# A two-layer decoder with routed experts on one core: the first nine expert blocks issued behind the first stream's last attention, six of them in one PSUM bank, with new issue orders

## The chip, the cores and the metric

The kernel runs on one core of one Trainium2 chip. The metric is the device time of one execution in microseconds (us), lower is better. The core has five engines that run side by side: PE (TensorE, matmuls), DVE (VectorE), ACT (ScalarE), POOL (GpSimd) and SP (SyncE, which issues DMAs). Each has a queue of its own and works through it strictly in order; they wait for each other on semaphores.

## The reference, cut to what matters

Tokens: 32 sequences of 64 with 128 features. Six sublayers run one after the other, each ending in a residual sum and a layer norm. The last one is a mixture of experts:

```python
x = _layernorm(x + _L0_attn_ref(...))      # causal attention, 16 heads of 8
x = _layernorm(x + _L0_xattn_ref(...))     # attention over ctx, normed heads
x = _layernorm(x + _L0_ffn_ref(...))       # fp4-quantized gated FFN
x = _layernorm(x + _L1_attn_ref(...))      # convolutions, linear attention, MLP
x = _layernorm(x + _L1_xattn_ref(...))     # causal attention over ctx
x = _layernorm(x + _L1_ffn_ref(...))       # experts

# _L1_ffn_ref
router_probs = softmax(residual @ W_router)                    # 8 experts
top_k_probs, top_k_idx = top_k(router_probs, 2)
top_k_probs = top_k_probs / (sum(top_k_probs) + 1e-08)
gate = silu(residual @ W_gate[e] + b_gate[e]); up = residual @ W_up[e] + b_up[e]
expert_out = (gate * up) @ W_out[e] + b_out[e]                 # 256 hidden
output = sum over e of expert_weights[e] * expert_out[e]
```

All is fp32.

## The kernel before, in words

The 2,048 tokens are four chunks of 512. Two streams, `first` and `second`, each take two of them in two turns, so that two chunks are in work at the same time. Each stream owns four of the eight PSUM banks (`h.ps`, banks 0 to 3 of its half) and its own SBUF tiles. On each engine three generators exist: the network of the first stream, the network of the second, and the expert blocks. A list of counts per engine, `ORDER`, says how many steps of each are issued in turn (`weave`, the third count is the blocks'); since the queues are in order, this list is the schedule. A step is what lies between two `yield`s.

A stream's turn ends with `causal_cross_attention` (four tiles: scores, row maxima, exponentials, transposes of the probabilities, mix with the values, projection, norm) and `routing`. Routing takes the logits (PE L941), the softmax and the two best experts (DVE L1709 to L1729), ranks the tokens of each expert with matmuls (L950, L953), writes each token's row with shares (L1736, L1739), then the token's place in its expert's list (L1751 to L1760); the counts so far are in `next_row` (L1755, semaphore step "taken"). The shares are transposed (PE L962), copied (ACT L1260) and mixed with the output bias (PE L967), and DVE adds this to the token's row (`h.acc`, L1763). POOL sends the rows to a table in HBM by indirect DMAs, eight for a stream's turn (L1998). `plan_blocks` (DVE L1800 to L1824) works out from the counts which expert and which 128 rows each block has.

There are 39 expert blocks of 128 rows. Their plan is made in three phases: blocks 0 to 8 are known once the first turn of both streams is counted, 9 to 16 after the first stream's second turn, 17 to 38 after the second's. For a block `b`: SP loads 128 rows (L536, six slots `xb`), PE transposes them (`turn`, L976), ACT copies (`take`, L1267), DVE copies the expert's weights (`weigh`, L1871; it loads the expert's number into a register first, L1867), PE projects (`gate_up`, L984, eight matmul passes into bank 1 or 2 in alternation), ACT applies Silu (`gate`, L1274), DVE multiplies with the up half (`hide`, L1879), PE makes the output (`out_part`, L998, bank 3), ACT scales it (`take_out`, L1284) and POOL sends it to HBM by an indirect DMA (L2007). DVE also works out the places for three blocks at a time (`pick`, L1839 to L1861). Between blocks 16 and 17 PE loads the sums so far into the second stream's banks (`add_base`, L1017). At the end the shares are read back, added (L1043) and normed.

The blocks use the first stream's tiles: `xb` lies in `first.probs`, the transposed rows, gates and hidden values in `first.pT`, the outputs in `first.qT`, the weights in `first.k4`, and PSUM banks 0 to 3 are the first stream's. In the kernel before, no block touches them before the first stream's last routing is over: SP and DVE wait for all of its `route_dve` steps, DVE also for its `route_pe` and `route_act`, and on PE block 0's projection stands behind the routing of both streams.

Of the kernel before, what the change touches and what calls it, by code (L numbers as in the profile page):

```python
# [26 lines left out]
ACT = mybir.ActivationFunctionType  # L27
# [4 lines left out]
P = 128  # L32
# [20 lines left out]
DEPTH, YDEPTH, WDEPTH, BATCH = 6, 4, 3, 3  # L53

# [38 lines left out]
def steps(*names):  # L93
# [49 lines left out]
    "act": (  # L143
# [11 lines left out]
    "dve": (  # L155
# [1994 lines left out]
```

## Time and profile before

| | us |
|---|---|
| median of 3 runs | 739.48 |
| lowest, highest | 736.78, 741.73 |
| span of the profiled execution | 763.12 |
| PE busy in it | 568.6 (75%) |
| DVE busy | 531.9 (70%) |
| ACT busy | 327.7 (43%) |
| POOL busy | 200.5 (26%) |

The profile is of one execution, and its times are positions on that execution's clock from the start of its span. PEld is the weight load of PE. "Granted clock" is the share of full speed that TensorE was allowed: 0.50 is 1.2 GHz and 1.00 is 2.4 GHz. "Issue" as the reason of a wait means that the profile shows nothing that the engine waited for, "remote" or "an unknown queue" that a semaphore came without a known sender close by.

### The profile page before, as it was taken

What the parts mean: (1) busy time and instruction counts of PE and PEld (TensorE: products, weight loads), DVE (VectorE), ACT (ScalarE), POOL (GpSimd) and SP (SyncE); (2) the same over time, 40 slices, a digit from 0 to 9 for tenths busy, and PEclk for the clock granted to TensorE, in tenths of its full rate; (3) what the DMA queues carried; (4) which work ended last, traced back from release to release, by engine and by line L of the source; (5) the groups of instructions that cost most, each with busy time, mean ns of one, the idle gap of its engine ahead of it and who ended that gap; (6) DMA issues with size and microseconds to landing.
All of it is one profiled execution on the core that took longest, in us unless ns stands there. A gap on an engine that the chain in (4) does not pass through costs nothing.

```text
span 763.1 us, 13948 instructions
## 1 busy us (share of the span) xinstructions
PE 568.6 (75%) x4890; PEld 393.2 (52%) x4890; DVE 531.9 (70%) x1520; ACT 327.7 (43%) x642; POOL 200.5 (26%) x312
## 2 busy tenths in 40 slices
PE   5787668756788688775975784667886987679984
PEld 2466546534455347442764463444542675567861
DVE  9667677888667667673686778996855767455633
ACT  2653445312474465142634451126744632344632
POOL 2204201201203502046043011121024034454543
PEclk9897669667699989687888797777997885599998
DMA  9993000000000000011000000000000001132215
GB/s 276 326 298 98 28 1 2 1 0 0 2 1 0 1 1 3 1 33 54 2 6 0 1 2 1 0 2 0 2 0 1 2 1 40 58 96 68 78 54 155
DMA packets 45556, 32.34 MB, mean 42 GB/s; under 512 B 4281, under 2 KB 43457, under 8 KB 45361
## 3 DMA queue, kind: packets, MB, share of 16 engines
q1 hardware_dynamic: 41104, 25.49, 12.1%
q0 software_dynamic: 2272, 4.92, 1.9%
q10 hardware_dynamic: 2112, 1.05, 0.5%
q8 instruction: 40, 0.66, 0.4%
q14 instruction: 28, 0.22, 0.1%
HBM read 13.83 MB, written 17.62 MB: 41 GB/s over the span
## 4 chain that ended last, share of the span: by engine, by line
PE 43%; DVE 32%; ACT 11%; issue 7%; POOL 4%; another core or an unknown queue 2%; DMA 1%; DVEq 0%; ACTq 0%; POOLq 0%
PE ps L643 5%; PE ps L984 5%; PE ps L624 5%; PE ps L687 5%; DVE s_row_max L1408 2%; PE ps L998 2%; ACT s_probs L1135 2%; DVE s_probs L1413 2%; DVE s_r L1377 2%; PE ps L655 2%; PE ps L906 1%; PE ps L911 1%; DVE s_st L1380 1%; DVE s_work L1367 1%
## 5 line engine op out<-in xcount | busy, mean ns | idle before, releaser
L1954 POOL TENSOR_TENSOR s_rs<-s_mv,eps 128x1 f32<-128x1 f32 x80 | 17.1, 215 | 349.3 <-DVE s_mv L1383 349.2
L1408 DVE TENSOR_REDUCE s_row_max<-ps 128x16 f32<-128x1024 f32 x48 | 58.7, 1222 | 62.3 <-PE ps L643 47.2
L1115 ACT ACTIVATE s_pT<-ps 128x512 f32<-128x512 f32 x96 | 55.5, 594 | 56.6 <-PE ps L624 44.2
L624 PE MATMUL ps<-tabs,s_probs 128*128 128x128 f32 x384 | 64.2, 302 | 19.8 <-ACT s_probs L1135 12.2
L643 PE MATMUL ps<-s_k,s_q 64*64 64x256 f32 x768 | 64.8, 451 | 13.5 <-ACT s_q L1085 9.9
L624 PEld LDWEIGHTS ps<-tabs,s_probs 128*128 128x128 f32 x384 | 45.8, 152 | 40.7 <-issue 19.9
L1135 ACT ACTIVATE s_probs<-s_probs 128x1024 f32<-128x1024 f32 x48 | 50.6, 1055 | 24.0 <-DVE s_probs L1413 23.7
L1413 DVE TENSOR_TENSOR s_probs<-ps,s_row_max 128x1024 f32<-128x1024 f32 x48 | 58.7, 1222 | 1.3
L687 PE MATMUL ps<-s_v,s_pT 128*64 128x18 f32 x1536 | 54.9, 216 | 3.5 <-issue 1.4
L687 PEld LDWEIGHTS ps<-s_v,s_pT 128*64 128x64 f32 x1536 | 51.0, 143 | 12.0 <-issue 11.0
L984 PE MATMUL ps<-s_pT,s_k 128*128 128x128 f32 x312 | 48.4, 304 | 3.8 <-issue 1.6
L1985 POOL TENSOR_SCALAR s_k<-s_kT,tabs 128x512 f32<-128x512 f32 x24 | 38.1, 1596 | 45.9 <-DVE s_kT L1442 28.8
L2007 POOL DMA_INDIRECT shares_io<-s_qT,y_row x39 | 38.0, 975 | 42.5 <-ACT s_qT L1284 38.1
L643 PEld LDWEIGHTS ps<-s_k,s_q 64*64 64x64 f32 x768 | 32.2, 156 | 31.1 <-issue 13.5
L984 PEld LDWEIGHTS ps<-s_pT,s_k 128*128 128x128 f32 x312 | 42.9, 213 | 8.4 <-issue 6.5
L1957 POOL TENSOR_TENSOR s_rs<-s_rs,minus_half 128x1 f32<-128x1 f32 x80 | 44.9, 565 | 5.2
L1879 DVE SCALAR_TENSOR_TENSOR s_pT<-ps,s_k,s_pT 128x128 f32<-128x128 f32 x78 | 23.7, 345 | 28.2 <-ACT s_pT L1274 19.8
L1274 ACT ACTIVATE s_pT<-ps,s_k 128x128 f32<-128x128 f32 x78 | 24.5, 367 | 37.7 <-PE ps L984 22.8
L1998 POOL DMA_INDIRECT rows_io<-s_work,s_slot x32 | 31.3, 977 | 16.7 <-issue 9.2
L1065 ACT ACTIVATE s_xT<-ps 128x512 f32<-128x512 f32 x20 | 11.9, 594 | 49.3 <-PE ps L603 24.4
L809 PE MATMUL ps<-gu_w,s_xT 128*128 128x352 f32 x64 | 30.8, 625 | 1.1 <-ACT s_xT L1065 1.1
L998 PE MATMUL ps<-wo,s_pT 128*128 x156 | 27.1, 298 | 5.6 <-ACT s_qT L1284 5.6
(288 smaller groups left out, 1247.8 us busy)
## 6 DMA issues: line engine op xcount, KB each, us to landing
rows_io<-zero_rows SPq DMA_DIRECT2D x9, 1152.0 KB, 11.9
s_probs<-rows_io SPq DMA_DIRECT2D x39, 72.0 KB
s_xin<-in_x SPq DMA_DIRECT2D x4, 256.0 KB, 4.1
s_cin<-in_ctx SPq DMA_DIRECT2D x4, 256.0 KB, 4.1
wgu<-in_wg SPq DMA_DIRECT2D x1, 1024.0 KB
wgu<-in_wu SPq DMA_DIRECT2D x1, 1024.0 KB
wo<-in_wo SPq DMA_DIRECT2D x1, 1024.0 KB
out_x<-s_work SPq DMA_DIRECT2D x4, 256.0 KB, 2.3
```

The lines of the kernel that those rows point to most:

```text
L624: ins = pe.transpose(h.ps[:, 2, tile(j)], h.probs[:, t % 2, 8 * part + 2 * j:8 * part + 2 * j + 2, :] .rearrange("p h k -> p (h k)"), ident)
L643: ins = pe.matmul(h.ps[S * b:S * b + S, half, 256 * side:256 * side + 256], h.q4[rows, side, S * sq:S * sq + S], h.k4[rows, sq, :, :].rear ...
L687: ins = pe.matmul(h.ps[S * b:S * b + S, 3, 18 * j:18 * j + 18], h.pT[:, t % 2, j, S * b:S * b + S], h.v2[:, 2 * t + b, 2 * j:2 * j + 2, :] ...
L984: ins = pe.matmul(ps[:, 1 + b % 2, tile(m)], wb[:, b % WDEPTH, tile(m)], xbT[:, b % 2, :], start=True, stop=True)
L998: ins = pe.matmul(ps[:, 3, 0:P], bhid[:, b % 2, tile(m)], wo[:, bass.ds(e, 1), m, :].rearrange("p e d -> p (e d)"), start=m == 0, stop=m == 1)
L1115: act.activation(h.pT[:, t % 2, 4 * part:4 * part + 4, :].rearrange("p j q -> p (j q)"), h.ps[:, 2, :], ACT.Copy).then_inc(h.pT_here.sem, 1)
L1135: act.activation(h.probs[:, u % 2, :, :], h.probs[:, u % 2, :, :], ACT.Exp).then_inc(h.exped.sem, 1)
L1408: dve.tensor_reduce(h.row_max[:, t % 2, :], s3, AX, ALU.max).then_inc(h.max_here.sem, 1)
L1413: dve.tensor_tensor(h.probs[:, t % 2, :, :], s3, h.row_max[:, t % 2, :].rearrange("p (h o) -> p h o", o=1).to_broadcast([P, H, S]), ALU.su ...
L1957: pool.tensor_tensor(h.rs[:, t % 2:t % 2 + 1], h.rs[:, t % 2:t % 2 + 1], minus_half[:, 0:1], ALU.pow).then_inc(h.rstd_here.sem, 1)
L1985: ins = pool.tensor_scalar(h.k4[:, :, m, :], seqs(h.kT[:, :]), tab("member")[:, m:m + 1], None, ALU.mult)
L2007: pool.indirect_dma_start(shares_io, bass.IndirectOffsetOnAxis(ap=y_row[:, g % 3, k:k + 1], axis=0), yb[:, b % YDEPTH, :], None).then_inc( ...
```

## The change

It does six things.

- SP's first load of a block waits for `first.p_turned` of the last turn (all probabilities of the first stream transposed) instead of `first.route_dve`.
- PE's first projection waits for `first.shifted` (banks 0 and 1 read), the first output for `first.summed` (bank 3 read), and projection 6 for all of the first stream's `route_dve`. ACT's first copy and DVE's first weighing wait for `first.mixed`.
- Blocks 0 to 5 all project into bank 1 (`NARROW = 6`), blocks from 6 on alternate as before. A projection therefore waits for the hide of the block before it up to block 6, and of the one two before from block 7 on.
- In its last turn, the first stream's shares are transposed and mixed in its bank 2 instead of 3, and the transposes wait for the step "taken" instead of "rows".
- `ewT` (the transposed shares) moves from `k4` to `work`, since `wb` needs its place.
- The four lists in `ORDER` are new throughout. On PE, `turn` of blocks 0 and 1 stands between the last tiles of both attentions, projection 0 directly behind the first stream's bias mix, and then, in turns with the second stream's ranks, shares and bias mix, projections 1 and 2. On DVE the weighings of blocks 0 and 1 stand inside the routings; the hide of block 0 stands in front of the larger part of the plan of blocks 9 to 16 and of the second stream's counts and slots, whose steps follow between the hides of blocks 0 to 5; the plan of the last phase ends behind the weighing of block 14 instead of 16. On POOL six of the first stream's sends come first, then the second stream's first, and then those left alternate with the blocks' own sends up to block 9; before, the sends of both streams came first but for three.

```diff
+NARROW = 6
@@ ORDER: all four lists are new @@
-            h.ewT = placed(h.k4, 3 * TOK, TOK)[0:EXPERTS, :]
+            h.ewT = placed(work, 3 * TOK, TOK)[0:EXPERTS, :]
+        def proj_bank(b):
+            return 1 if b < NARROW else 1 + b % 2
+        def bank_free(b):
+            return b if b <= NARROW else b - 1
+        def share_bank(h):
+            return 2 if h is first and h.turn == PASSES - 1 else 3
@@ sync, blocks_of_experts @@
-                        sp.wait_ge(*first.route_dve.at(0, PASSES))
+                        sp.wait_ge(*first.p_turned.at(0, PASSES))
@@ tensor, routing @@
-                pe.wait_ge(*h.route_dve.at(ROUTE_DVE["rows"]))
+                pe.wait_ge(*h.route_dve.at(ROUTE_DVE["taken" if share_bank(h) == 2 else "rows"]))
-                    ins = pe.transpose(h.ps[0:EXPERTS, 3, tile(t)], h.pay[:, t, P:P + EXPERTS], ident)
+                    ins = pe.transpose(h.ps[0:EXPERTS, share_bank(h), tile(t)], h.pay[:, t, P:P + EXPERTS], ident)
-                    ins = pe.matmul(h.ps[:, 3, tile(t)], h.ewT[:, tile(t)], bout[:, :], start=True, stop=True)
+                    ins = pe.matmul(h.ps[:, share_bank(h), tile(t)], h.ewT[:, tile(t)], bout[:, :], start=True, stop=True)
@@ tensor, gate_up and out_part @@
-                    if b >= 2:
-                        pe.wait_ge(b_hid, b - 1)
+                    if b == 0:
+                        pe.wait_ge(*first.shifted.at(0, PASSES))
+                    if b == NARROW:
+                        pe.wait_ge(*first.route_dve.at(0, PASSES))
+                    if bank_free(b):
+                        pe.wait_ge(b_hid, bank_free(b))
-                        ins = pe.matmul(ps[:, 1 + b % 2, tile(m)], ...)
+                        ins = pe.matmul(ps[:, proj_bank(b), tile(m)], ...)
-                    if b >= 1:
+                    if b == 0:
+                        pe.wait_ge(*first.summed.at(0, PASSES))
+                    else:
                         pe.wait_ge(yb_here, b)
@@ scalar, blocks_of_experts; ps[:, proj_bank(b)] in gate as well @@
                 yield
+                act.wait_ge(*first.mixed.at(0, PASSES))
                 take(0)
@@ vector, blocks_of_experts; ps[:, proj_bank(b)] in hide as well @@
-                dve.wait_ge(*first.route_dve.at(0, PASSES))
-                dve.wait_ge(*first.route_pe.at(0, PASSES))
-                dve.wait_ge(*first.route_act.at(0, PASSES))
+                dve.wait_ge(*first.mixed.at(0, PASSES))
                 weigh(0)
```

## Rows read from the trace of the kernel before

**Rows 1.** Busy time by stretch: stretch, length, busy us (instructions) by engine, clock, DMA.

```profile
625.00:640.00 15.00, 11.31 (x60) 8.86 (x58) 10.08 (x71) 2.61 (x6) 2.17 (x6) 0.50 0.01 2
...
650.00:660.00 10.00, 3.49 (x14) 2.96 (x14) 2.65 (x12) 2.70 (x10) 4.76 (x5) 0.50 0.17 54
...
690.00:745.00 55.00, 49.32 (x339) 39.31 (x338) 28.80 (x105) 25.99 (x94) 25.36 (x26) 1.00 0.25 72
```

**Rows 2.** The chain that ended last, 600 to 763 us: start, us, what.

```profile
647.86 1.71 PE ps L984 x8
649.56 5.34 issue
...
675.16 2.23 another core or an unknown queue
...
678.04 1.53 another core or an unknown queue
...
691.23 3.44 PE ps L1017 x8
```

**Rows 3.** Timeline, the handover: start, us, engine, line, operation, [idle before <-releaser].

```profile
613.13 0.63 PE L624 MATMUL ps<-tabs,s_probs 128*128 128x128 f32 x4 [0.23 <-ACT s_pT L1115]
...
634.41 0.19 DVE L1739 TENSOR_TENSOR s_work<-s_spread 128x32 f32<-128x32 f32 x1
...
635.43 1.01 PE L962 MATMUL ps<-tabs,s_work 128*8 128x128 f32 x4
...
636.69 0.16 DVE L1755 TENSOR_TENSOR next_row<-next_row,ps 128x8 f32<-128x8 f32 x1
...
637.12 2.07 PE L967 MATMUL ps<-bout,s_k 8*128 8x128 f32 x8 [0.68 <-ACT s_k L1260]
...
639.62 1.06 POOL L1998 DMA_INDIRECT rows_io<-s_work,s_slot  x1 [7.53 <-DVE s_slot L1760]
...
641.48 0.17 DVE L1805 TENSOR_TENSOR fp_gu<-fp_gu,taken 128x8 f32<-128x8 f32 x1
...
642.44 0.21 DVE L1811 TENSOR_REDUCE fp_gu<-fp_gu 128x8 f32<-128x56 f32 x1
...
645.66 1.98 PE L984 MATMUL ps<-s_pT,s_k 128*128 128x128 f32 x8
...
646.20 1.28 ACT L1274 ACT_TABLE_LOAD   x1
...
652.37 0.63 ACT L1274 ACTIVATE s_pT<-ps,s_k 128x128 f32<-128x128 f32 x2 [4.88 <-remote]
...
655.01 0.96 POOL L1998 DMA_INDIRECT rows_io<-s_work,s_slot  x1 [0.30 <-issue]
```

**Rows 4.** The weighing's lines: line, engine, operation, count, ns min/median/max, first and last start.

```profile
L1867 DVEq TENSOR_LOAD <-plan_expert x21: 298/304/547, 644.0 to 698.8; - x21
L1867 DVEq FUSED_REGOPS x21: 190/190/216, 644.6 to 699.2; - x21
...
L1871 DVE TENSOR_SCALAR s_k<-wgu x39: 428/431/679, 645.0 to 733.5; 128x516 f32 x39
```

**Rows 5.** Timeline of single blocks: block 3, then projections 6 and 38.

```profile
660.10 2.05 PE L984 MATMUL ps<-s_pT,s_k 128*128 128x128 f32 x8 [0.63 <-ACT s_pT L1267]
...
662.19 0.63 ACT L1274 ACTIVATE s_pT<-ps,s_k 128x128 f32<-128x128 f32 x2 [2.13 <-PE ps L984]
...
663.11 0.61 DVE L1879 SCALAR_TENSOR_TENSOR s_pT<-ps,s_k,s_pT 128x128 f32<-128x128 f32 x2 [1.22 <-PE ps L998]
...
666.73 1.13 PE L984 MATMUL ps<-s_pT,s_k 128*128 128x128 f32 x8
...
734.24 1.13 PE L984 MATMUL ps<-s_pT,s_k 128*128 128x128 f32 x8 [0.21 <-issue]
```

**Rows 6.** Busy time by stretch in the first turn's routing (columns as in rows 1).

```profile
341.00:347.00 6.00, 6.00 (x48) 3.14 (x41) 3.00 (x3) 1.74 (x3) 4.69 (x5) 0.51 0.17 52
347.00:363.00 16.00, 6.90 (x55) 3.54 (x54) 4.31 (x5) 3.09 (x5) 9.61 (x10) 0.82 0.15 51
```

More of the change, by code:

```diff
@@ L980, in gate_up @@
                     pe.wait_ge(b_weights, b + 1)
-                    if b >= 2:
-                        pe.wait_ge(b_hid, b - 1)
+                    if b == 0:
[4 more added lines that the diff above has]
+                        pe.wait_ge(b_hid, bank_free(b))
                     for m in range(2 * EM // P):
-                        ins = pe.matmul(ps[:, 1 + b % 2, tile(m)], wb[:, b % WDEPTH, tile(m)], xbT[:, b % 2, :], start=True, stop=True)
+                        ins = pe.matmul(ps[:, proj_bank(b), tile(m)], wb[:, b % WDEPTH, tile(m)], xbT[:, b % 2, :], start=True, stop=True)
                     ins.then_inc(b_proj, 1)
@@ L1259, in routing @@
                 act.wait_ge(*h.route_pe.at(ROUTE_PE["shares_turned"]))
-                act.activation(h.ewT[:, :], h.ps[0:EXPERTS, 3, 0:TOK], ACT.Copy).then_inc(h.route_act.sem, 1)
+                act.activation(h.ewT[:, :], h.ps[0:EXPERTS, share_bank(h), 0:TOK], ACT.Copy).then_inc(h.route_act.sem, 1)
             def blocks_of_experts():
@@ L1273, in gate @@
                     for m in range(EM // P):
-                        ins = act.activation(bsg[:, b % 2, tile(m)], ps[:, 1 + b % 2, tile(m)], ACT.Silu,
+                        ins = act.activation(bsg[:, b % 2, tile(m)], ps[:, proj_bank(b), tile(m)], ACT.Silu,
                                              bias=wb[:, b % WDEPTH, 2 * EM + m:2 * EM + m + 1])
@@ L1762, in routing @@
                 dve.wait_ge(*h.route_pe.at(ROUTE_PE["bias_mix"]))
-                dve.tensor_tensor(h.acc[:, :, :], h.ps[:, 3, :].rearrange("p (t d) -> p t d", d=P), h.pay[:, :, 0:P],
+                dve.tensor_tensor(h.acc[:, :, :], h.ps[:, share_bank(h), :].rearrange("p (t d) -> p t d", d=P), h.pay[:, :, 0:P],
                                   ALU.add).then_inc(h.route_dve.sem, 1)
@@ L1878, in hide @@
                     for m in range(EM // P):
-                        ins = dve.scalar_tensor_tensor(bhid[:, b % 2, tile(m)], ps[:, 1 + b % 2, EM + P * m:EM + P * m + P],
+                        ins = dve.scalar_tensor_tensor(bhid[:, b % 2, tile(m)], ps[:, proj_bank(b), EM + P * m:EM + P * m + P],
                                                        wb[:, b % WDEPTH, 2 * EM + 2 + m:2 * EM + 3 + m], bsg[:, b % 2, tile(m)], ALU.add, ALU.mult)
```

110 rows, old and new, of the table ORDER are left out of this document.

## The prediction

> **What bounds the kernel now.** I read the busy times by stretch first, then the chain of waits, then the timeline around the place where the network hands over to the expert blocks. The stretches [rows 1] show three regimes. From 625 to 640 us both streams route: PE runs at a granted clock of 0.50 (1.2 GHz) and DVE is busy 10.1 of 15 us with tiny steps. From 650 to 660 us nothing is full: PE 3.5 of 10 us, DVE 2.7, ACT 2.7. From 690 to 745 us the clock is 1.00 (2.4 GHz) and PE is busy 49.3 of 55 us, so there PE is the bound. The first projection starts at 645.66 and the last (block 38) at 734.24; block 3 starts at 660.10 [rows 3, 5], so 35 blocks take 74.1 us, 2.1 us each, but the first three take 14.4 us. The chain of waits names the hole: 5.34 us of idle after block 1's projection, 2.23 and 1.53 us near 676 us that end with no known releaser, and 3.44 us of the eight matmuls that bring the base into PSUM between blocks 16 and 17 [rows 2]. So the change can win only between about 635 and 665 us; what it wins there is kept, since PE works back to back behind it.
>
> The hole is odd: block 0's projection ends at 647.64, the table load for Silu at 647.48, yet ACT begins the gate at 652.37 [rows 3]. The wait between them is on PE's own semaphore, which arrived 4.7 us late. At that time POOL issues 13 row sends back to back, 639.62 to 655.97. In the first turn it is alike: while 15 sends run from 340.6 us on, PE keeps 6.0 of 6 us busy at first, then 6.9 of 16 [rows 6]. I call this late release; it goes with a long run of sends, and begins some 7 us into one.
>
> **The change part by part.**
> 1. *Loads and turns.* SP loads blocks behind the last transpose of the first stream's probabilities instead of behind its last routing step, so the first six 72 KB loads move from 641 us to about 615 us, just behind those transposes (613.13 to 613.76 [rows 3]), where POOL sends nothing. The transposes of blocks 0 and 1 and their copies (PE 0.47 and ACT 0.28 us each, cold) now stand inside the tail of both attentions, in front of work that is on the path. Cost +0.5 us, between 0 (they fit in gaps) and 1.5.
> 2. *The first stream's routing.* Its last shares go through bank 2, which is free only when the row counts were taken (L1755, ends 636.85) instead of when the rows are there (L1739, ends 634.60) [rows 3]. With the weighing of block 0 put into DVE before it, I put that at 637.1. From the shares' transposes (L962) to the bias mix (L967) it is 1.69 us and the mix lasts 2.07 [rows 3]: it ends at 640.9, and block 0's projection, now next on PE and no longer behind the second stream's mix, starts there: 4.8 us earlier than 645.66. The Silu table load is hidden, since ACT is free from about 639 us.
> 3. *One bank for six blocks.* Each of projections 1 to 6 must wait until the block before has been hidden. Block 3 shows such a round, cold: projection from 660.10, gate from 662.19, hide from 663.11 to 663.72 [rows 5]: 3.62 us. Warm it is 1.13 + 0.63 + 0.61 us and small gaps, 2.5 us.
> 4. *DVE.* The new order puts 24 steps of routing and planning, 7 of picking, 5 weighings and 5 hides between the hides of blocks 0 and 5. A step costs 0.24 us (from 641.48 to 642.44, four of them [rows 3]); a weighing 1.1 us with its register load (0.30 + 0.19 + 0.43 us and gaps [rows 4]); a hide 0.61 [rows 5]; the accumulate with the mix adds 0.4. Sum 31 x 0.24 + 5 x 1.1 + 5 x 0.61 + 0.4 = 16.4 us. These steps are not new work: before, they ran ahead of the first hide or in the hole, and cost nothing there. Now they are beside the blocks.
>    Block 0 is hidden at 640.9 + 3.6 = 644.6 (DVE's own queue gives the same). Projection 6 then starts between 644.6 + 16.4 = 661.0 (DVE decides) and 644.6 + 5 x 3.62 = 662.7 (the one bank decides, cold), and was at 666.73 [rows 5]: 4.0 to 5.7 us earlier. The second stream's mix (2.07 us) now stands between projections 1 and 2 and speaks for the late end. I take 4.3 us.
> 5. *Late releases.* Those gains are against a trace with 5.34 us of hole in it, while my rounds have none. The 16 sends are still issued, and blocks now run beside all of them. In the new POOL order the second stream's first send waits for slots that DVE writes only behind the hide of block 2, so the run is six sends long, then pauses, then mixes with the blocks' own sends. Bounds: nothing returns (0) or all of it (+5.3). Since the 7 us of grace cover the first run and not what follows, I take half, +2.7.
> 6. *Plan of the last phase.* It ends two blocks earlier in DVE's order. Hidden anyway: PE loads the base for 3.44 us between blocks 16 and 17 [rows 2] and block 17's transpose follows directly. I take 0; if that cover were gone it would be worth about 2 us, a block's pace.
> 7. *Orders elsewhere.* Nearly every line of the four orders is rewritten, but step by step they are close: no step of PE changes its place by more than five among 631, ACT's by four; DVE's by up to 20 among 1,326 and POOL's by up to 12. Sum 0, with +-4 us for what a reordered DVE does to two streams over 625 us.
>
> Sum: +0.5 - 4.3 + 2.7 = -1.1 us against the profiled 763.1, so 762.0. That execution is 23.6 us above the median of the runs. I can't say where those lie; if the late releases are partly of the profiled execution alone, the old hole is smaller in the runs. The difference is carried over as it stands: 739.48 - 1.1 = 738.4, and I say **738 us**.
>
> The Trainium skill ("SBUF — State Buffer", SBUF: two separate sides) says that GpSimd and VectorE share a port pair under an exclusive lock, so that a DVE fp32 copy in a fast mode keeps POOL from writing descriptors, and puts a POOL DMA overlapped by one at about 3.1 us instead of 0.62. By its figures the nine weighings beside sends would cost some 2.5 us each on POOL. The traced sends beside the weighings at 645.02 and 646.57 kept their 1.27 us rhythm, so the trace does not show this size.
>
> **Rivals.**
> A. *The hole is closed (chance 0.20).* The long run of 13 sends is what makes the semaphores late, and the new order breaks it at six. Then term 5 is 0 and the two later stalls (2.23 and 1.53 us) go too, as B's last sends are spread: 738.4 - 2.7 - 3.8 = 732; if the denser PE also brings the clock to 1.00 sooner than at 664 us, rounds of 2.5 us and DVE's 16.4 decide, 1.5 more: 730. For it: early loads don't collide. Against: the stall at 677 us comes after only four indirect DMAs in a row.
> B. *Blocks in the way (0.20): slower.* The second stream's routing now queues behind projections 0 and 1, gates 0 and 1 and three hides, each of which can be released late. Two or three late releases of 4.7 us, each in a loop where one bank lets nothing overlap, are 9.4 to 14 us, less the 4.3 won: 743 to 749, say 745. It decides from the point where more than one such release falls in the six one-bank rounds.
> C. *It does nothing (part of the forecast's neighbourhood, 0.15).* In a run with no late releases before, block 0 would have been gated at 647.7 and hidden by 649.0, projection 2 would have followed at once and projection 3 one cold round later, near 652.7; one more cold round and two of the steady pace of 2.1 put projection 6 near 660.5 on the trace's clock, as early as the new order brings it. Only term 1 and a little of the denser DVE queue are left: 740.
> D. *The rewritten orders decide (0.10),* 4 us or more to either side, 733 or 744.
> The forecast itself, 735 to 741, has 0.35.
>
> **How the numbers follow.** The range takes A's 730 and B up to 747: 729 to 747, leaving out 0.1 on each side. About 1%, 7.4 us, is what a measurement of this kernel tells from no change: under 732.1 is faster, over 746.9 slower. Faster: A, most of its reach, and a part of D and of the forecast's tail, 0.23. Slower: the upper half of B and of D with a little for what I don't see, 0.17. Within 1%: 0.60.
>
> **What would show it.** Right: the first L984-type projection near 641 with the first stream's mix directly before it; the distance from projection to projection 3.0 to 3.6 us for blocks 0 to 6 and 2.1 behind; projection 6 near 662 on the old clock. Term 3 is wrong if DVE is idle before those hides, term 4 if it is not and the rounds are shorter than 3 us. Term 5 shows as ACT waits of over 1 us that begin after a projection has ended, while POOL sends. The prediction is wrong if the network's end has moved by more than 4 us before the blocks, or if the second stream's sends land so late that block 17 waits for its load.

## The result, and the profile after

| | us |
|---|---|
| kernel before, median | 738.32 |
| changed kernel, median of 4 runs | 758.04 |
| lowest, highest of them | 754.86, 760.19 |
| ratio, 95% interval | 1.027, 1.022 to 1.032 |
| span of its profiled execution | 756.5 |

The change costs 19.7 us. The prediction, 738 us with a range of 729 to 747, was wrong in its sign and outside its range.

One thing has to be settled before the traces are compared. The profiled execution of the changed kernel (756.5) agrees with its runs. That of the kernel before (763.12) stood 23.6 us above its own median, and some 2 us more as a run, since a run's time is 2.0 us above its span (758.46 and 756.5 for the changed kernel's profiled run). So the changed kernel's trace is 6.6 us shorter than the trace of before, although the kernel is 19.7 us slower. Busy time by stretch of the changed kernel, at the places that answer to [rows 6] and [rows 1] (columns as there):

```profile
356.00:372.00 16.00, 14.24 (x233) 9.96 (x233) 11.87 (x14) 10.47 (x16) 6.79 (x8) 1.00 0.11 38
635.70:650.70 15.00, 9.86 (x52) 7.66 (x51) 11.47 (x78) 4.06 (x8) 4.45 (x8) 0.62 0.02 7
660.70:670.70 10.00, 6.45 (x51) 5.88 (x51) 7.58 (x35) 4.15 (x16) 7.67 (x8) 1.00 0.21 65
683.40:738.40 55.00, 49.58 (x351) 40.51 (x349) 29.74 (x108) 26.80 (x98) 29.36 (x31) 1.00 0.26 78
```

Both holes of the trace of before are gone. Beside the sends of the first turn PE is busy 14.2 of 16 us (6.90 in [rows 6]), and among the first blocks 6.5 of 10 us (3.49 in [rows 1]). The steady part is as it was, 49.6 of 55 us at a clock of 1.00.

The timeline of the handover in the changed kernel (start, us, engine, line, operation, [idle before <-releaser]). L1773 is L1751 of before, where the first stream's rows are known; L1003 is L984; L1295 is L1274; L1901 is L1879:

```profile
645.20 0.18 DVE L1773 TENSOR_TENSOR s_row_of<-ps,next_row 128x32 f32<-128x32 f32 x1
...
649.40 2.08 PE L1003 MATMUL ps<-s_pT,s_k 128*128 128x128 f32 x8
...
651.51 0.62 ACT L1295 ACTIVATE s_pT<-ps,s_k 128x128 f32<-128x128 f32 x2 [2.87 <-PE ps L1003]
652.17 0.61 DVE L1901 SCALAR_TENSOR_TENSOR s_pT<-ps,s_k,s_pT 128x128 f32<-128x128 f32 x2
...
652.93 1.20 PE L1003 MATMUL ps<-s_pT,s_k 128*128 128x128 f32 x8 [0.16 <-DVE s_pT L1901]
...
655.57 1.13 PE L1003 MATMUL ps<-s_pT,s_k 128*128 128x128 f32 x8 [0.26 <-DVE s_pT L1901]
...
666.35 1.13 PE L1003 MATMUL ps<-s_pT,s_k 128*128 128x128 f32 x8 [0.90 <-DVE s_pT L1901]
```

The handover does what the diff says. Block 0 is projected 4.2 us behind L1773, behind 11.1 us in the trace of before, and the six blocks follow in one-bank rounds, each projection released by the hide ahead of it. But L1773 stands at 645.20, where L1751 stood at 634.5: the network arrives 10.7 us late, although the trace of before has 12.8 us of late semaphores ahead of that place (e1 below). Against ordinary executions of the old order it is twice as much: the profiled executions of e10 and e14 below, with spans of 735.1 and 735.9 us, have that operation at 623.41 and 623.82, so 21.8 and 21.4 us earlier. The loss lies ahead of everything that the prediction worked out.

To compare handovers, take that operation, the first stream's row places, as the mark. "Cold" stands for a granted clock of 0.50 (1.2 GHz), "warm" for 1.00. Per profiled execution, in us (first column: where it starts on the clock; the others: from there to the projections of four blocks and to the end of the span):

| kernel | mark | block 0 | block 6 | block 9 | block 17 | end |
|---|---|---|---|---|---|---|
| before, first profile | 634.5 | 11.1 | 32.2 | 37.8 | 60.9 | 128.6 |
| before, profiled again (e1) | 632.7 | 11.2 | 22.5 | 28.1 | 45.8 | 111.9 |
| changed | 645.2 | 4.2 | 21.2 | 27.4 | 46.2 | 111.3 |

### The profile page after: what moved, and what is told of

Read it like the earlier page. It is cut to its first block, busy times and chain, and to the rows that moved or that the text cites. A ratio compares the mean times of both kernels' runs of the same rounds, so it can differ in the third digit from the quotient of the medians.

```text
span 756.5 us, 13948 instructions
## 1 busy us (share of the span) xinstructions
PE 568.0 (75%) x4890; PEld 391.5 (52%) x4890; DVE 526.6 (70%) x1520; ACT 326.8 (43%) x642; POOL 199.9 (26%) x312
## 4 chain that ended last, share of the span: by engine, by line
PE 49%; DVE 27%; ACT 11%; issue 6%; POOL 3%; DMA 2%; SPq 0%; DVEq 0%; POOLq 0%; ACTq 0%
PE ps L702 6%; PE ps L658 5%; PE ps L639 5%; PE ps L1003 3%; DVE s_row_max L1430 2%; PE ps L625 2%; PE ps L921 2%; PE ps L1019 2%; PE ps L926 2%; DVE s_probs L1435 2%; PE ps L670 2%; ACT s_probs L1156 2%; PE ps L824 1%; DVE s_r L1399 1%; ACT s_q L1106 1%
## 5 line engine op out<-in xcount | busy, mean ns | idle before, releaser
L1974 POOL TENSOR_TENSOR s_rs<-s_mv,eps 128x1 f32<-128x1 f32 x80 | 16.4, 208 | 338.1 <-DVE s_mv L1405 337.9
L639 PE MATMUL ps<-tabs,s_probs 128*128 128x128 f32 x384 | 62.3, 293 | 23.0 <-ACT s_probs L1156 20.0
L658 PE MATMUL ps<-s_k,s_q 64*64 64x256 f32 x768 | 61.1, 442 | 10.1 <-ACT s_q L1106 10.1
L639 PEld LDWEIGHTS ps<-tabs,s_probs 128*128 128x128 f32 x384 | 44.0, 147 | 41.8 <-ACT s_probs L1156 29.1
L2005 POOL TENSOR_SCALAR s_k<-s_kT,tabs 128x512 f32<-128x512 f32 x24 | 37.8, 1587 | 48.7 <-DVE s_kT L1464 29.5
L1003 PE MATMUL ps<-s_pT,s_k 128*128 128x128 f32 x312 | 44.2, 286 | 6.3 <-DVE s_pT L1901 4.2
L1003 PEld LDWEIGHTS ps<-s_pT,s_k 128*128 128x128 f32 x312 | 38.7, 195 | 11.4 <-issue 5.9
L2027 POOL DMA_INDIRECT shares_io<-s_qT,y_row x39 | 38.0, 974 | 23.6 <-ACT s_qT L1305 20.0
L658 PEld LDWEIGHTS ps<-s_k,s_q 64*64 64x64 f32 x768 | 30.6, 154 | 25.6 <-ACT s_q L1106 11.2
L1295 ACT ACTIVATE s_pT<-ps,s_k 128x128 f32<-128x128 f32 x78 | 24.4, 364 | 31.6 <-PE ps L1003 31.6
L670 PE MATMUL ps<-mats,s_headsT 128*128 128x128 f32 x96 | 24.7, 353 | 12.2 <-DVE s_heads L1448 9.4
L1901 DVE SCALAR_TENSOR_TENSOR s_pT<-ps,s_k,s_pT 128x128 f32<-128x128 f32 x78 | 23.7, 346 | 11.8 <-ACT s_pT L1295 8.1
```

Of the source, the lines that this page charges most:

```text
L639: ins = pe.transpose(h.ps[:, 2, tile(j)], h.probs[:, t % 2, 8 * part + 2 * j:8 * part + 2 * j + 2, :] .rearrange("p h k -> p (h k)"), ident)
L658: ins = pe.matmul(h.ps[S * b:S * b + S, half, 256 * side:256 * side + 256], h.q4[rows, side, S * sq:S * sq + S], h.k4[rows, sq, :, :].rear ...
L670: pe.matmul(h.ps[:, 3, P:2 * P], h.headsT[:, u % 2, :], mat(w_out), start=True, stop=True).then_inc(h.projected.sem, 1)
L1003: ins = pe.matmul(ps[:, proj_bank(b), tile(m)], wb[:, b % WDEPTH, tile(m)], xbT[:, b % 2, :], start=True, stop=True)
L2027: pool.indirect_dma_start(shares_io, bass.IndirectOffsetOnAxis(ap=y_row[:, g % 3, k:k + 1], axis=0), yb[:, b % YDEPTH, :], None).then_inc( ...
```

## The experiments

Two questions are told apart: where the network loses its time (e1, e3, e5 to e7, e9 to e11), and where the gain of the handover goes (e1, e2, e4, e8, e12 to e14). The theories before the first runs: **U**, the new orders of the network ahead of the last attentions cost it; **B**, the blocks stand in the way of the second stream's routing (rival B of the prediction); **E**, the edits cost it, whatever the order.

### e1: the kernel before, profiled again

No edit.

> The kernel before, unchanged, profiled once more. Theory U (the new orders of the first 590 us cost about 20 us, and the execution that the prediction read was an untypical one, with some 12 us of late semaphores at 342 to 362 us and some 12 more at 647 to 665 us): time 739, and if this profile agrees with its runs its span is about 737, the step that stood at 362 us in the first profile stands near 350, and projection 38 near 710. Theory B (the blocks stand in the way of the second stream's routing, so the loss lies behind 620 us): the time is 739 too, and against this profile the changed kernel loses nothing before 620 us and some 20 us behind it.

Measured: median 738.11 us over 10 runs, against 737.90 of before. The profiled execution has a span of 744.5; its run, 746.54, is the longest of the ten (the shortest is 733.90) and has the lowest mean clock of them, 0.828. Its busy times by stretch, at the places of the two holes, then its timeline:

```profile
355.00:371.00 16.00, 14.76 (x226) 10.35 (x223) 13.27 (x16) 10.82 (x16) 10.45 (x11) 0.99 0.17 56
...
648.00:658.00 10.00, 9.48 (x76) 8.99 (x77) 8.20 (x35) 5.99 (x24) 7.78 (x8) 0.96 0.29 89
```

```profile
643.82 1.97 PE L984 MATMUL ps<-s_pT,s_k 128*128 128x128 f32 x8
...
645.82 0.62 ACT L1274 ACTIVATE s_pT<-ps,s_k 128x128 f32<-128x128 f32 x2 [0.18 <-PE ps L984]
```

The same kernel, the same 16 sends, and no hole: block 0 is gated 0.03 us after its projection ended, not 4.73 us as in [rows 3]. The late semaphores belong to the one execution that was profiled first. The longest of them stands in the first turn: an 11.3 us wait of ACT from 350.75 on, without a known sender. Operation by operation, the first profile loses 12.8 us against this one between 340 and 362 us and 16.7 us behind the mark; this one in turn is 9.0 us slower ahead of 340 us, where its granted clock is lower. The expected place of projection 38, 710, was 715.2, by that lower clock. That e1 is a long run does not touch the comparison behind the mark: e10 and e14 have the old order there too, and put block 0 at 11.1, block 6 at 22.5, block 9 at 28.0 and the end at 111.7 and 112.1.

### e2 to e4: orders and edits apart

```diff
# e2 (base: changed kernel)
-ORDER = the new lists
+ORDER = the lists of before
# e3 (base: before)
-ORDER = the lists of before
+ORDER = steps of each stream's network ahead of its last attention as in the new lists, the rest as before
# e4 (base: changed kernel)
-ORDER = the new lists
+ORDER = steps of each stream's network ahead of its last attention as before, the rest as in the new lists
```

> The changed kernel with all its new waits, the one bank and the new place of the shares, but with the four issue orders of the kernel before. Theory U: 739 to 742, since the network is issued as before; the first block is projected behind both routings and only the six blocks in one bank can cost 1 to 3 us. Theory E (the edits themselves cost it: one bank for six blocks, the shares' wait for the row counts): 750 to 758. Theory B: like U here, since no block stands ahead of the second stream's routing.

> The kernel before (old waits, two banks) with the new issue order for every step of the network that stands ahead of the last attention of each stream, and the old order from there on. Theory U: 756 to 762, all of the loss and nothing of the gain. Theory B and theory E: 737 to 742, as the kernel before.

> The changed kernel with the old issue order for every step of the network that stands ahead of the last attention of each stream, and the new order from there on (both last attentions, both routings, the blocks). Theory U: 733 to 738, the gain of the handover without the loss upstream, and so a version better than both. Theory B and theory E: 755 to 760, as the changed kernel.

| | median us | ratio to before | mark | end behind the mark |
|---|---|---|---|---|
| e2, edits, old orders | 744.08 | 1.012 (1.002 to 1.022) | 621.7 | 119.0 |
| e3, new orders upstream alone | 759.66 | 1.029 (1.021 to 1.037) | 644.0 | 112.6 |
| e4, edits and new orders behind | 739.64 | 1.000 (0.995 to 1.006) | 621.2 | 113.5 |

Theory U holds. The kernel before with nothing but new orders upstream has all of the loss (+21.8 us), and the changed kernel without them can't be told from before. B falls twice: e4 has the blocks in front of the second stream's routing and loses nothing, and in the changed kernel the second stream's rows (second L1773, 652.82) follow the first's after 7.6 us, as they do in e1 (7.8). E is right for a smaller sum: with the old orders the edits cost 6.2 us (interval 0.2% to 2.2%), most of it in the one bank. There block 0 starts 1.2 us later behind the mark than in e1, and block 6 8.8 us later: the rounds of the first blocks are 4.0, 3.5 and 3.8 us (projections at 634.01, 637.97, 641.47, 645.23), almost wholly cold (mean clock 0.55). e4 did not gain the 4 us that theory U as written promised.

### Where the network loses it: e6, e7, e9

Comparing e3 with e4, operation by operation, the delay of e3 grows at many places, roughly from 2 us at 160 to 5 at 240, 9 at 320, 15 at 380, 19 at 460 and 25 at 540; at the mark it is 22.8. The execution of e4 has a high mean clock (0.872), and 2.3 us of this are its lead over e10. Theory **M**: many local changes of order, each paid where it stands. Theory **S**: one place, or a state carried along.

```diff
 ORDER (base: before; all four engines)
# e6
+steps of the first turn of both streams as in the new lists
# e9
+steps of the second turn ahead of its last attention as in the new lists
# e7
+steps of the linear block, in both turns, as in the new lists
```

> The kernel before with the new order for all steps of the first turn (both streams, its routing included) and the old order for everything else. Theory M (the loss is made of many local changes of order, each paid where it stands): 746 to 750, the 9 to 10 us that the changed kernel is late at 340 us. Theory S (one place, or the state the second turn is entered in, carries the loss): either 738 or 758.

> The kernel before with the new order for the steps of the second turn ahead of its last attention, and the old order for the first turn and for the rest. Theory M (many local places, each paid where it stands): what is left of the 21.5 us of the whole upstream order when the first turn's 5.9 us are taken off, 15 to 16 us, so 751 to 755. If the two halves do not add up (under 748 or over 757) the turns act on each other, through the clock or through how far one stream is ahead of the other.

> The kernel before with the new order for the steps of the linear block alone, in both turns. Theory M: between the changed and the former order the stretches that hold these blocks differ by 3.7 us in the first turn and 3 to 4 in the second, so 743 to 747. Theory S: as the kernel before, 738, since the rest of the order is the old one.

| | median us | above before |
|---|---|---|
| e6, first turn | 744.01 (ratio 1.010, 1.004 to 1.016) | 5.9 |
| e9, second turn | 752.84 (1.017, 1.010 to 1.023) | 14.5 |
| e7, linear block, both turns | 742.81 (1.007, 1.004 to 1.010) | 4.7 |

The two halves add up, 5.9 + 14.5 = 20.4 against 21.8 for both, and one sublayer of five holds 4.7. M holds; e6 came out 2 us under its expected range, e7 0.2 us. Each part costs less than 2%, but all three intervals lie above 1.

What a place looks like is seen in the busy times of three pairs of stretches that hold the same work. e4 (old order), then e3 (new order):

```profile
265.00:300.00 35.00, 30.18 (x444) 20.75 (x443) 24.21 (x42) 21.66 (x33) 3.32 (x7) 0.90 0.01 1
300.00:340.00 40.00, 29.01 (x225) 18.30 (x225) 29.66 (x128) 13.98 (x28) 10.56 (x15) 0.81 0.05 14
365.00:400.00 35.00, 24.01 (x280) 20.42 (x280) 29.16 (x92) 13.17 (x28) 15.07 (x21) 0.90 0.01 4
```

```profile
270.10:306.70 36.60, 30.64 (x444) 20.94 (x443) 24.97 (x41) 21.62 (x33) 3.29 (x7) 0.91 0.01 1
306.70:349.80 43.10, 34.52 (x215) 21.86 (x211) 29.89 (x128) 12.24 (x26) 10.47 (x15) 0.68 0.05 13
375.80:415.00 39.20, 28.49 (x275) 24.30 (x275) 27.05 (x92) 12.60 (x26) 16.19 (x23) 0.70 0.03 9
```

In the first pair the clock is alike (0.90, 0.91) and 1.6 us go, 1.1 of them as idle time of PE. In the two others 3.1 and 4.2 us go and the granted clock falls from 0.81 to 0.68 and from 0.90 to 0.70: PE is busy 5.5 and 4.5 us longer with the same work (the counts differ a little, since stretches cut it at different places and some matmul records are missing).

The runs show how much goes with the clock. Over 90 runs of before, all those beside the experiments and e1's, the mean granted clock went from 0.828 to 0.865 and the time followed it by -3.2 us for each 0.01, with 741.5 at 0.84. The changed kernel's four runs (mean clock 0.8375) lie 15.5 us above that line; the other 4 us go with the lower clock (mean of before 0.849). This is a division, not a cause: whether the clock falls first or the waits come first is not shown by it. The same line has something to say on e4. Its ten runs had a higher clock (0.857) and lie 5.0 us above the line, so that its equal time is not an equal handover.

### e5 and e11: one swap of neighbours

```diff
 ORDER["dve"] (base: before), second turn, linear block
-first stream: second tap of the convolution; second stream: norm statistics
+second stream: norm statistics; first stream: second tap of the convolution
```

> The kernel before with two neighbours on DVE exchanged, once: in the second turn's linear block the second stream's norm statistics (four L1596, 0.88 us) are issued ahead of the first stream's second convolution tap (L1589), as the new order has it. In the new order's traces this stands at the head of a place where 3 us go. Theory Q (queue and clock together): ACT's next operation on that tile comes 0.7 us later, PE waits for it over 2 us instead of 1.5, falls to a granted clock of 1.2 GHz, its next two pairs of 128x512 matmuls take 2.07 and 1.91 us instead of 1.13 and 1.02, and DVE's L1620 starts 1.5 to 1.8 us later than before against the tap ahead of the swap (6.1 us behind it before). Theory N (a swap of neighbours costs at most its own length): 0 to 0.7 us later and no slower matmuls. In both the whole kernel stays within its noise, 736 to 742; the trace decides.

The timeline of e4, which has the old order here (L1609 is the tap, L1616 the statistics):

```profile
509.00 0.74 DVE L1605 SCALAR_TENSOR_TENSOR s_work<-s_work,cols 128x504 f32<-128x504 f32 x1 [0.46 <-ACT s_work L1226]
509.78 0.74 DVE L1609 SCALAR_TENSOR_TENSOR s_work<-s_work,cols 128x504 f32<-128x504 f32 x1
510.44 0.88 DVE L1616 BATCH_NORM_STATS2 s_nst<-ps 128x6 f32<-128x128 f32 x4
...
511.24 1.13 PE L864 MATMUL ps<-s_work,mats 128*128 128x512 f32 x2 [1.46 <-ACT s_work L1232]
512.21 1.02 PE L865 MATMUL ps<-s_work,mats 128*128 128x512 f32 x2
...
515.12 0.69 DVE L1640 SCALAR_TENSOR_TENSOR s_kT<-s_k,s_kT 128x512 f32<-128x512 f32 x1 [0.53 <-ACT s_k L1238]
```

The timeline of e5 (the same operations stand at L1584, L1595, L1588, L850, L851 and L1619):

```profile
513.42 0.74 DVE L1584 SCALAR_TENSOR_TENSOR s_work<-s_work,cols 128x504 f32<-128x504 f32 x1 [0.45 <-ACT s_work L1206]
514.08 0.88 DVE L1595 BATCH_NORM_STATS2 s_nst<-ps 128x6 f32<-128x128 f32 x4
514.88 0.72 DVE L1588 SCALAR_TENSOR_TENSOR s_work<-s_work,cols 128x504 f32<-128x504 f32 x1
...
516.32 1.50 PE L850 MATMUL ps<-s_work,mats 128*128 128x512 f32 x2 [2.30 <-ACT s_work L1212]
517.62 1.92 PE L851 MATMUL ps<-s_work,mats 128*128 128x512 f32 x2
...
520.57 0.69 DVE L1619 SCALAR_TENSOR_TENSOR s_kT<-s_k,s_kT 128x512 f32<-128x512 f32 x1 [1.83 <-ACT s_k L1218]
```

Theory Q holds in its mechanism. The tap is 0.7 us later, PE waits 2.30 instead of 1.46 us, and then works at 1.2 GHz: a pair that took 1.02 us takes 1.92. DVE's next dependent operation comes 7.15 us behind the tap ahead of the swap instead of 6.12, a loss of 1.0 us (1.5 to 1.8 was expected). All 16 profiled executions have these two pairs of matmuls. In ten of them PE waited 1.29 to 1.65 us ahead of the first pair, and the pairs took 1.12 or 1.13 and then 1.02 us; in the six others (changed, e3, e5, e7, e9, e11) it waited 1.99 to 2.65 us, and they took 1.44 to 2.08 and then 1.62 to 1.92 us. A little further on two more pairs run slowly, at 531.06 and 532.76 for 1.91 and 1.64 us where e4 has 1.02, and from 528.6 on e4's clock every DVE operation is 2.7 us later than before the swap, to 0.01 us. So one swap of two neighbours, which moves 0.7 us of work, cost 2.7 us at its place. Not all of it stays. Against e10 and e14, which have the old order here and behind it, e5 is 0.7 and 0.3 us late ahead of the swap, 3.4 and 3.0 behind it, but 2.1 and 1.7 at the mark (625.55 against 623.41 and 623.82): 1.2 us came back, between 573 and 614 us on e10's clock. The run itself, 741.26, can't show so little.

e11 takes the swap out of the changed kernel again, and with it POOL's order at the start of the second turn:

```diff
 ORDER (base: changed kernel)
-"dve", that place: statistics, tap
+"dve", that place: tap, statistics
-"pool", first turn's row sends and the next norms: new order
+"pool", first turn's row sends and the next norms: order of before
```

> The changed kernel with two places of its order put back: the DVE swap of e5, and POOL's order of the first turn's row sends and the norms beside them (the place of e10). Theory M: 2.7 us for the first, as e5's trace shows, and 2 to 4 us for the second come back of the 19.7: 751 to 755. Theory S (whatever is put back, the streams fall into the same slower pattern): 757 to 760.

Measured: 754.01 us, 4.0 below the changed kernel, within the expected range; but the four runs of each overlap (750.36 to 758.72, 754.86 to 760.19), so the trace has to carry it. The delay against e4 jumps by 1.5 us at the place of the swap, where e3's jumps by 4.4: 2.9 us came back there. Directly, the changed kernel is 0.5 us ahead of e11 up to the swap and 2.7 behind it from then to the mark (645.20 against 642.48): here nothing of it is made up. At POOL's place, near 370 us, the delay of e11 against e4 jumps by 4.0, as e3's does, and its distance from the changed kernel stays as it was (0.5 us): nothing came back.

### e10: a move that costs nothing

```diff
 ORDER["pool"] (base: before), start of the second turn
-first stream: scale of tile 1, variance of tile 2; second stream: last send, variance of tile 0
+second stream: last send, variance of tile 0; first stream: scale of tile 1, variance of tile 2
```

> The kernel before with one move on POOL: at the start of the second turn the two steps that turn the first stream's second tile's variance into its scale (the second half L1962 of one norm and the first L1959 of the next) stand behind the second stream's last row send and its first norm instead of ahead of them, as in the new order. POOL then waits for the second stream's statistics first, which come 5 to 6 us after the first stream's are ready. Theory M: the first stream's tile is normed 5 to 6 us later and the kernel loses 2 to 4 us: 740 to 743. Theory N (a chain that is late in one stream is covered by the other stream): 737 to 739.

Measured: 738.24 us against 738.34. The scale of tile 1 is there at 372.58 instead of near 368.6, 4 us late, and no later operation moves. Theory N was right here and M was wrong on this place: this late step was covered, by the other stream's work as theory N has it; what covered it was not looked at. What costs 4 to 5 us near 370 us in the new order has not been found.

### Where the gain of the handover goes: e8, e12, e13, e14

```diff
# e8 (base: e4)
-NARROW = 6
+NARROW = 3
# e12 (base: e4)
-ORDER["pool"] behind the last attention: new
+ORDER["pool"] behind the last attention: as before
# e13 (base: e4) and e14 (base: before)
-DEPTH, YDEPTH, WDEPTH, BATCH = 6, 4, 3, 3
+DEPTH, YDEPTH, WDEPTH, BATCH = 6, 8, 3, 3
-        yb = first.qT[:, :].rearrange("p (k d) -> p k d", d=P)
+        yb_four = [b[:, :].rearrange("p (k d) -> p k d", d=P) for b in (first.qT, first.kT)]
```

> The kernel of e4 (old order up to the last attentions, changed tail) with three blocks in one bank instead of six, so that blocks 3, 4 and 5 alternate between two banks and block 3 waits for all of the first stream's routing steps. Theory D (DVE's interleaved routing and planning steps set the 2.6 to 3.5 us rounds of blocks 1 to 8): 738 to 741, no gain against e4. Theory O (the one bank sets them): each of three rounds shortens by 0.5 to 1 us, 736 to 738 against e4's 739.6.

> The kernel of e4 (old order upstream, changed tail) with POOL's queue in the old order: all sixteen row sends but the last ahead of the first output send of a block. Theory L (a long run of indirect sends makes semaphores late, as in the first profile): PE or ACT waits of over 1 us whose releaser had ended before, and 742 to 752. Theory Y (only the blocks' outputs are late): outputs wait for their four buffers, projections do not, 739 to 742. If neither is seen the interleaving on POOL was worth nothing: 738 to 740.

> The kernel of e4 (old order upstream, changed tail) with eight buffers for the blocks' outputs instead of four (the second four lie in the first stream's kT). Theory P (in the changed tail POOL sends without a pause from 635 to 656 us, 1.26 us each, and the four buffers make ACT wait for it: the output of block 12 waits for the transfer of block 8, gate 15 stands behind it, and so does block 17): ACT's wait of some 3.4 us in front of the output of block 12 goes, blocks 16 and 17 are projected 2.5 to 3.5 us earlier, and the median is 736 to 737 against 739.6. Theory D (DVE's order sets it): 739 to 740.

> The kernel before with the same eight output buffers and nothing else. Theory P: in the re-profiled run of before the chain runs over PE from block 9 on and not over POOL, so the buffers hide nothing there: 737 to 738.5, no gain. If this is 735 to 736, the buffers and not the issue orders are where the tail can be improved, in both kernels.

From the mark, as in the table above, with the medians and, as base, before's 737.9 to 738.4 us:

| kernel | block 0 | block 6 | block 9 | block 17 | end | median us |
|---|---|---|---|---|---|---|
| e4 | 4.2 | 21.1 | 27.3 | 46.7 | 113.5 | 739.64 |
| e8, three blocks in one bank | 4.2 | 20.1 | 29.3 | 48.8 | 114.5 | 739.65 |
| e12, POOL's old order | 4.2 | 21.2 | 32.2 | 50.8 | 117.7 | 744.32 |
| e13, eight outputs | 4.2 | 21.2 | 27.4 | 45.0 | 111.5 | 738.66 |
| e14, before with eight outputs | 11.1 | 22.5 | 28.0 | 45.6 | 112.1 | 737.99 |

Against e1 (11.2, 22.5, 28.1, 45.8, 111.9) the new handover leads by 7 us at block 0, by 1.3 at block 6, by 0.8 at block 9 and by nothing at block 17. Part of even this is paid ahead of the mark. From 552 us on e10's clock to the mark e4 loses 1.5 us against e10, and e8, e12 and e13 lose 1.0 to 1.4, while e1, e2 and e14, with the old order there, lose nothing (0.04 us at most). With 1.8 us more from the mark to the end e4 is 3.3 us behind e10 in all. The changed kernel, against e3 with the same order upstream, loses 0.6 us ahead of the mark and gains 1.3 behind it. Leaving the bank earlier (e8) gains 1 us at block 6 and loses it again: theory O is not borne out. The chain of waits of e13 says what holds block 9, in both kernels the first block of the second phase (start, us, what):

```profile
650.17 0.31 DVE fp_gu L1839
651.73 0.35 DVE fp_gu L1841
652.56 1.94 DMA s_probs<-rows_io
654.54 0.33 PE ps L997
```

Its rows can only be loaded when that phase is planned and the first stream's rows are in the table, 25.7 us behind the mark here, 26.5 in e1. Blocks 0 to 8 were early for nothing. In e1 the chain enters block 9 by the last row sends and the load of their rows.

e12 shows what the new order on POOL is needed for. ACT in e12, at the output of block 4:

```profile
656.01 0.37 ACT L1308 ACTIVATE s_qT<-ps,s_pT 128x128 f32<-128x128 f32 x1 [5.04 <-DMA shares_io<-s_qT,y_row]
...
656.43 0.63 ACT L1298 ACTIVATE s_pT<-ps,s_k 128x128 f32<-128x128 f32 x2
```

With nine sends in a row in front of them (642.3 to 652.4) the blocks' outputs wait for their four buffers, the gate of block 7 stands behind that on ACT, and block 8 is projected at 657.85. It costs 4.7 us against e4 by the medians (1.008, 1.005 to 1.011, against 1.000, 0.995 to 1.006) and 4.2 us behind the mark. Neither of the two theories has this right: the buffers do reach the projections (Y said not), and no semaphore is late in the sense of L. The same wait is in e4 in small, 2.12 us at 661.01. Eight buffers take it away, block 17 comes 1.7 us earlier and the end 2.0. The median is 1.0 us lower, not the 3 expected of theory P, and the ratios to before (1.000 and 1.001) don't show even that. In the kernel before they change nothing. No kernel run here is measurably faster than the kernel before.

## Why the prediction was wrong, point by point

- **What bounds the kernel now: the row was read rightly, its weight was not.** The hole of 5.34 us [rows 2] and the thin first-turn stretch [rows 6] were there, and belonged to that execution. It stood 23.6 us above the median. The prediction wrote that it could not say where those lie, while [rows 3] and [rows 6] held them: 12.8 us in the first turn and 16.7 us in the handover (the sum, 29.5, is more than 23.6; executions also differ in other stretches, as e1 ahead of 340 us). Rival C's picture of a run without late releases was right: it put projection 6 14.8 us behind projection 0, and e1 shows 11.3.
- **Term 1** (early loads and turns, +0.5, 0 to 1.5): the range holds, but in e4 the value is at its upper end. The new order of the last attentions, in which the turns stand, delays the mark by 1.0 to 1.5 us in e4, e8, e12 and e13, and by 0.6 in the changed kernel against e3. What part of it the turns and copies have was not tried by itself.
- **Term 2** (block 0 starts 4.8 us earlier): the right mechanism, undersized. It is 6.9 us, 4.2 behind the mark instead of 11.1.
- **Term 3** (one bank, 2.5 us warm, 3.62 cold): right in its sizes. In the changed kernel the rounds are 3.5, 2.6, 3.0 and three of 2.6 us; in e2, cold, 3.5 to 4.0.
- **Term 4** (DVE's 16.4 us from hide 0 to projection 6): it took 13.6. Block 6 comes 11.1 us earlier than in the trace of before, where 4.0 to 5.7 were worked out, but 1.3 earlier than in e1. The comparison with a trace full of waits was the fault, not the working.
- **Term 5** (half of the late releases return, +2.7): wrong. None of 15 other profiled executions shows them, with or without the blocks' sends between: the gates of blocks 0 to 6 begin within 0.05 us of the end of their projections in all of them.
- **Term 6** (last plan, 0): nothing speaks against it. Block 17's delay has other reasons.
- **Term 7** (orders elsewhere, 0 with 4 us to either side): **this is the step that failed.** It measured +20 to +22 us (e3 +21.8, e6 and e9 together +20.4). The argument was that no step of PE moves by more than five places. A displacement in places says nothing of time: e5 exchanges two neighbours and loses 2.7 us at that place, e10 moves four steps by two places and loses nothing. Nor was zero the right centre: every larger part that was tried (e6, e7, e9) lost time, and none gained. The trace had the hint and it was not looked at: where PE's groups stand behind waits of 0.5 to 1.5 us for ACT or DVE, as in the linear block of e4, the swap of e5, which makes one of those later by 0.7 us, was on the path.
- **Rival A** has nothing to close in a run without the hole. **Rival B** had the right sign with the wrong cause (e4); its 743 to 749 also starts from two bases, as 9.4 to 14 less 4.3 on 739.5 is 744.6 to 749.2. **Rival C** describes the handover: -0.6 us behind the mark for the changed kernel against e1, +1.6 for e4. **Rival D** named the cause, gave it 0.10 and 4 us, and split it evenly between gain and loss.
- **What would show it wrong** held: the prediction said that the network's end moved by more than 4 us would break it, and it moved by 10.7 us against the first profile, 12.5 against e1, and 21.8 and 21.4 against e10 and e14.

The sends beside the weighings, for which the prediction named the Trainium skill ("SBUF — State Buffer", SBUF: two separate sides), can be read again: the send at 653.75 of the changed kernel, beside the weighing at 653.67, took 1.18 us, and its neighbours 0.96; in e4 the send at 629.69, beside the weighing at 629.62, took 1.19. That is 0.2 us, not the 2.5 us estimated from the page's figures.

Left open: which changes of order carry the other 17 us, besides the one of e5; the 4 to 5 us near 370 us above all. PE, DVE, ACT or POOL alone in the new order was not tried, so which engine's list costs most is not known. And what made the semaphores late in one execution was not seen again, so it could not be tried.

## What to carry to other kernels

- If the profiled execution stands well above the median of the runs, find its extra time first, and do not argue from it: a second profile of the unchanged kernel is the cheapest experiment. What a change removes from a wait that only one execution has is worth nothing.
- In this kernel the price of a new order was not told by how far steps move. Rewriting a balanced order elsewhere in the kernel has to be costed for itself, with its own experiment (new order in one part, old in the rest), before what it makes room for.
- An early start is worth only what is left of it at the next wait for data. Here nine blocks came up to 7 us earlier and the tenth had to wait for rows and plan that did not move.

## What the runs showed of the hardware that was not expected

- Two kernels with the same order run alike to the hundredth: e1, e2 and e4 keep their distance from each other constant within 0.1 us from 475 to 555 us. What they differ by comes in single steps of 0.3 to 1.6 us, most of them ahead of 340 us, the last between 400 and 445 (e1 is 10.2 us behind e4 at 340 and 13.0 from 445 on). So a trace can show a loss of 2.7 us that medians can't.
- A longer wait of PE was paid for again behind it: after 2.30 us instead of 1.46 us of idle (0.84 more), the next pairs of 128x512 matmuls took 1.50 and 1.92 us instead of 1.13 and 1.02 (1.27 more), at 1.2 instead of 2.4 GHz. The 16 profiled executions fall into the same two groups there.
- Semaphores that came late, by 4.7 us at the first gate and in one wait of 11.3 us in the first turn, in one execution and in none of the 15 others.
